# Attention kernel: key tiles in six sets of 2, 3, 3, 2, 3 and 3 in place of eight pairs, stack loads issued behind a set's last tile

## The chip, the core and the metric

One core of a Trainium2 chip runs the program. The metric is the device time of one execution in microseconds. TensorE (PE in the rows; its weight loads PEld) multiplies, VectorE (DVE) and ScalarE (ACT) read its results from the eight PSUM banks, GpSimd (POOL) adds tiles, SyncE (SP), ACT and POOL issue DMAs.

## What is computed

```python
xn = layernorm(x)                      # x: 4 x 2048 x 512
q, k, v = heads(xn @ Wq.T + bq)/sqrt(32), heads(xn @ Wk.T + bk), heads(xn @ Wv.T + bv)   # 16 heads of 32
attn = softmax(q @ k.T)                # 2048 x 2048 for each of 4 * 16 = 64 heads
att = (attn @ v) @ Wo.T + bo
ffn = tanh(xn @ W @ A1 @ A2 + b)
out = x + att + ffn
```

## The kernel before

Three stages follow each other: the weights, the projections (queries and keys split in two parts of reduced precision and stacked on 96 rows, written to DRAM), and attention, `build_attend`, which the change is in. The attention of 64 heads takes most of the time. PE runs them in a loop of four heads per turn (15 turns) and the last four written out.

**The work of a head.** The 2048 keys are 16 key tiles of 128 (`kt`, 0 to 15), the 2048 queries four blocks of 512 (`q`). `scores` (L1122) computes a tile's scores for one block into one of three banks (`st_bank`); ACT takes their exponential into a tile `probs` (`exps`, L901). `use` (L1128) multiplies a whole exponential tile by the values into `pv_bank`, with weights of 32 columns, four blocks spread over the array's four column strips; the scores use 128 columns. So PE alternates between a stretch of 128-column score matmuls and a stretch of 32-column ones.

**The row maximum.** The exponential needs each query's maximum beforehand. `max_scores` (L1095) computes the scores a second time, queries on the rows, for a head that comes later, into one of four banks (`sm_bank`); DVE reduces each bank to a column (`maxima`, L999: a *read* below). A head has 64 such units, numbered `k`. The two kinds stand in turn: for each tile and block `both_scores` issues one maximum matmul, then one score matmul. The maxima run four tiles ahead: at tiles 0 to 11 stand units 16 to 63 of the next head, at tiles 12 to 15 units 0 to 15 of the head after. After unit 63 DVE reduces the columns to `row_max` (L1016), PE turns it (`turn_max`, L1104), DVE negates it (`negate`, L970) and SP loads it as row 97 of the query stack.

**The banks.** The table `SM_TURN` deals the units, the turned maximum (`"max"`) and the bank of the row sums (`"sum"`) to the four banks in turn; a maximum matmul waits until DVE has read what its bank held before, four places earlier (`sm_before`). A score matmul waits for the exponential three units earlier (`st_units_before`), one place being left free (`ST_SKIP`) and one for DVE's scaling (`SPARE_AFTER`: unit 2 of each head waits for `context_ready`).

**The order on PE.** Tiles go in pairs: the scores (with maxima) of two tiles, 8 maxima and 8 scores in turn, then `use` of the two tiles before:

```python
for p in range(CUT // 2, (KT if more >= 2 else END_TILE) // 2):
    both_scores(h, r, 2 * p, to_turn, more)
    both_scores(h, r, 2 * p + 1, to_turn, more)
    use(h, r, 2 * p - 2)
    use(h, r, 2 * p - 1)
```

After tiles 8 and 9 of the next head, `add_up` sums a head's exponentials over the keys. They have been added before: some tiles by POOL (L827), some by DMAs that POOL issues and that add to `dma_sum` (`join`, L838; `merge`, L846). ACT copies the sums and the product (`copy_sums`, `copy_pv`, L908); DVE inverts the sums after a head's 64 maxima (`invert`, L975 and L978) and scales after unit 15 (`scale`, L982 and L987). ACT also issues the loads of stacks three heads ahead (`load`, L299 and L305), one each after tiles 6, 7, 9, 10, 12, 13 and 15 (`LOAD_AT`).

Of the kernel before, what the change touches and what calls it, by code (L numbers as in the profile page):

```python
# [26 lines left out]
KT = SEQ // P  # L27
# [3 lines left out]
GROUP = 4  # L31
ROWS = 3 * DH
MROW = ROWS
SM_BANKS, ST_BANKS = 4, 3
UNITS = KT * QB
PER_TILE = UNITS // KT
AHEAD = 4
TURN_UNIT = 8
BEGIN = 16
SUM_UNIT = 56  # L40
SCALED = 15
ST_SKIP, ST_SLOTS = 24, 66
CUT = 10
LOAD_AT = [6, 7, 9, 10, 12, 13, 15]


CHAINS = [[0, 2, 5, 8, 10, 13]]
# [9 lines left out]
END_TILE = 12  # L57
# [5 lines left out]
LAST_CONTEXT = (BATCH - 1) * TB  # L63


SM_TURN = [*range(TURN_UNIT), "max", *range(TURN_UNIT, SUM_UNIT), "sum", *range(SUM_UNIT, UNITS), None, None]


MAX_FROM = 10
# [24 lines left out]
def sm_place(what):  # L94
    return SM_TURN.index(what) % SM_BANKS

# [29 lines left out]
SPARE_BEFORE = max(u for u in range(UNITS) if st_place(u) == spare_place())  # L126
SPARE_AFTER = min(u for u in range(UNITS) if st_place(u) == spare_place())

assert ST_SKIP % (2 * PER_TILE) == 0 and ST_SLOTS % ST_BANKS == 0 and SCALED + 1 == AHEAD * PER_TILE
assert UNITS == 64 and len(SM_TURN) % SM_BANKS == 0 and st_slot(UNITS - 1) == ST_SLOTS - 2  # L130


# [502 lines left out]
def build_attend(nc, dram, out, first):  # L635
# [3 lines left out]
    with ExitStack() as own:  # L639
# [241 lines left out]
        @block.scalar  # L881
        def _(act):
            for s in (probs_ready, pv_copied, sums_copied):
                act.sem_inc(s, PRIME)

            def exps(h, r, kt):

                for q in range(QB):
                    if q == 0 and kt in SLOT:
                        old, back = tile_before(kt)  # L890
                        act.wait_ge(tile_used, PRIME + h * KT - back * KT + old + 1)
                        if not back and isinstance(h, int) and h == LAST:
                            if old in LAST_POOL:
                                act.wait_ge(pool_added, PRIME + h * POOL_ADDS + max(1, LAST_POOL.index(old)))
                        elif old in POOL_TILES:
                            act.wait_ge(pool_added, PRIME + h * POOL_ADDS - back * POOL_ADDS + adds_after(old))
                        elif old != kt and not (back and isinstance(h, int) and h == 0):
                            before, place = (h - 1, (r + 1) % 2) if back else (h, r % 2)
                            act.wait_ge(joined[place], landed(before, CHAINS[0].index(old)))
                    act.wait_ge(scores_ready, h * UNITS + kt * QB + q + 1)  # L900
                    nc.scalar.activation(tile_at(r, kt)[:, q * BLK:(q + 1) * BLK],  # L901
                                         score_bank(h, kt * QB + q), ACT.Exp,
                                         scale=SCALE).then_inc(probs_ready, 1)

            def copy_bank(h, r, bank, copies, ready, value, copied):
                act.wait_ge(ready, value)
                act.wait_ge(context_ready, PRIME + h - 1)
                nc.scalar.activation(copies[r % 2][:], bank[:], ACT.Copy).then_inc(copied, 1)  # L908

            def copy_pv(h, r):  # L910
                copy_bank(h, r, pv_bank, pv_copy, tile_used, PRIME + h * KT + KT, pv_copied)

            def copy_sums(h, r):
                bank = last_sum if isinstance(h, int) and h == LAST else sum_bank
                copy_bank(h, r, bank, sum_copy, sums_ready, PRIME + h + 1, sums_copied)

            def high(n, par):
                act.wait_ge(ctx_loaded[par], (n // 2) * DMA + DMA)
                act.wait_ge(res_ready, PRIME + n * JT - JT)
                nc.scalar.activation(ctx_hi[par], ctx_in[par], ACT.Copy).then_inc(hi_ready, 1)  # L920

            def load(h, r, i):

                if i < len(PARTS):
                    load_part(act, dram, h, i, q_st[r], k_st[r], head_loaded[r])
                elif r % 2:
                    load_v(act, dram, h - 1, v_sb[r // 2], v_loaded[r // 2])

            for kt in range(CUT):
                exps(0, 0, kt)  # L930
                if kt == LOAD_AT[0]:
                    act.wait_ge(first["v_stored"], V_STORED)
                if kt in LOAD_AT:
                    load(GROUP - 1, GROUP - 1, LOAD_AT.index(kt))

            def body(h, r, more, following):
                for kt in range(CUT, KT):
                    exps(h, r, kt)
                    if kt in LOAD_AT and more >= GROUP - 1:
                        load(h + GROUP - 1, (r + GROUP - 1) % GROUP, LOAD_AT.index(kt))  # L940
                if more:
                    for kt in range(CUT):
                        exps(following, (r + 1) % GROUP, kt)
                        if kt == 1:
                            copy_pv(h, r)
                        if kt in LOAD_AT and more >= GROUP:
                            load(h + GROUP, r, LOAD_AT.index(kt))
                        if kt == CUT - 1:
                            copy_sums(h, r)
                else:  # L950
                    copy_pv(h, r)
                    high(2, 0)
                    high(3, 1)
                    copy_sums(h, r)

            heads(act, body)
            for n in range(4, EARLY_BLOCKS + 2):
                high(n, n % 2)
            block_pairs(act, lambda n, par, ahead: high(n + 2, par), EARLY_BLOCKS, BLOCKS - 2)

        @block.vector
        def _(dve):
# [30 lines left out]
            def maxima(s, k, units, sums_of):  # L993

                if units:
                    if k == 0:
                        dve.wait_ge(row_max_ready, PRIME + s)
                    dve.wait_ge(max_scores_ready, s * UNITS + k + 1)
                    nc.vector.tensor_reduce(part_max[:, k:k + 1], sm_bank[:, sm_place(k)], AX.X,  # L999
                                            ALU.max).then_inc(max_scores_read, 1)  # L1000
                if k == SCALED and sums_of is not None:
                    scale_in_spare(*sums_of)

# [4 lines left out]
                        negate(s - 1)  # L1008
                    maxima(s, k, units, sums_of)

            def rest(s, units=True, sums_of=None):
                for k in range(BEGIN, UNITS):
                    maxima(s, k, units, sums_of)
                if units:
                    dve.wait_ge(max_scores_read, PRIME + s * UNITS + UNITS)
                    nc.vector.tensor_reduce(row_max[:], part_max[:].rearrange("p (q b) -> p q b", b=QB), AX.X,  # L1016
                                            ALU.max).then_inc(row_max_ready, 1)
                if sums_of is not None:
                    invert(*sums_of)

            dve.sem_inc(max_row_ready, 1)
            rest(1)
# [20 lines left out]

            def body(h, r, more, following):
                if more >= 3:
                    rest(following + 1, sums_of=(h, r))
                    begin(following + 2, sums_of=(h, r))
                elif more == 2:
                    rest(following + 1)
# [28 lines left out]
        def _(pe):  # L1078
# [100 lines left out]
                    scores(h, r, kt, q)  # L1179

            pe.sem_inc(turned_ready, 1)
            for p in range(CUT // 2):
                both_scores(0, 0, 2 * p, 1, 2)
                both_scores(0, 0, 2 * p + 1, 1, 2)
                if p:
                    use(0, 0, 2 * p - 2)
                    use(0, 0, 2 * p - 1)

            def end_of_heads():

# [12 lines left out]
            def body(h, r, more, following, to_turn):  # L1203
                if more == 0:
                    return
                r1 = (r + 1) % GROUP
                for p in range(CUT // 2, (KT if more >= 2 else END_TILE) // 2):
                    both_scores(h, r, 2 * p, to_turn, more)
                    both_scores(h, r, 2 * p + 1, to_turn, more)
                    use(h, r, 2 * p - 2)  # L1210
                    use(h, r, 2 * p - 1)
                if more == 1:
                    end_of_heads()
                if more >= 2:
                    for p in range(CUT // 2):
                        both_scores(following, r1, 2 * p, to_turn + 1, more - 1)
                        both_scores(following, r1, 2 * p + 1, to_turn + 1, more - 1)
                        if p == 0:
                            use(h, r, KT - 2)
                            use(h, r, KT - 1)  # L1220
                        else:
                            use(following, r1, 2 * p - 2)
                            use(following, r1, 2 * p - 1)
                        if p == CUT // 2 - 1:
                            add_up(h, r, more)

            def output_part(n, par, j):
                pe.wait_ge(res_ready, PRIME + n * JT + j - JT + 1)
# [92 lines left out]
```

## Time and profile before

| | us |
|---|---|
| median of 3 executions | 4086.81 |
| lowest and highest | 4084.3, 4092.52 |
| the profiled execution | 4089.26 |
| its span in the trace | 4087.4 |

TensorE's granted clock is 0.998 of full over the span. The span's last instruction ends 1.9 us short of the profiled execution's time. In the trace a timeline row gives start, duration, engine, line, operation, tile written and read, and a count where like instructions were merged; in brackets stands the idle time before and what ended it. PE's matmuls are pipelined, so the distance between two starts is their cost, not the duration shown.

### The profile page before, as it was taken

To read this page: it belongs to the slowest core of one execution; us is meant where nothing else is said; L and a number is where in the kernel's file an instruction comes from. 1 tells how busy PE (TensorE), PEld (TensorE's weight loads), DVE (VectorE), ACT (ScalarE), POOL (GpSimd) and SP (SyncE) were. 2 spreads that over 40 slices of the span, in tenths; PEclk is the share of its full clock that TensorE was granted. 3 is DMA by queue.
4 is the path that set the end of the run, shared out by engine and by line. 5 is a ranking of instruction groups with operands and counts; after the bars stand their busy time and mean duration, and the time that the engine had idled before them with its cause. 6 is when DMAs were issued, how large, how long until landed. Compare 5 with 4: busy or idle time off the path is not lost.

```text
span 4087.4 us, 77851 instructions
## 1 busy us (share of the span) xinstructions
PE 4044.5 (99%) x21280; PEld 2493.3 (61%) x21280; DVE 3075.7 (75%) x5122; ACT 2367.1 (58%) x4515; POOL 3164.7 (77%) x1108
## 2 busy tenths in 40 slices
PE   8999999999999999999999999999999999999999
PEld 6888888755555555555555555555555555555477
DVE  4344333788888888888888888888888888888734
ACT  2222122167677677777676777776776767676621
POOL 1222222289999999999999999999999999999920
PEclk9999999999999999999999999999999999999999
DMA  4444444568888888888888888888888888888767
GB/s 173 157 170 159 153 151 159 174 148 168 176 180 176 179 170 179 173 177 174 175 178 178 176 175 175 174 171 174 178 179 178 171 176 175 177 175 177 171 211 257
DMA packets 245348, 714.80 MB, mean 175 GB/s; under 512 B 87281, under 2 KB 88305, under 8 KB 184433
## 3 DMA queue, kind: packets, MB, share of 16 engines
q0 software_dynamic: 54288, 395.34, 49.9%
q1 hardware_dynamic: 107648, 201.88, 14.5%
q10 hardware_dynamic: 83040, 113.01, 10.2%
q8 instruction: 186, 3.05, 0.3%
q14 instruction: 186, 1.52, 0.1%
HBM read 178.00 MB, written 136.31 MB: 77 GB/s over the span
## 4 chain that ended last, share of the span: by engine, by line
PE 63%; DMA 11%; issue 4%; POOL 2%; ACT 1%; POOLq 0%; ACTq 0%; DVE 0%; DVEq 0%
PE sm_bank L1095 20%; PE st_bank L1122 18%; PE pv_bank L1128 18%; DMA dma_sum<-pool_sum 6%; DMA dma_sum<-probs 5%; PE sm_bank L289 3%; POOL pool_sum L827 2%; PE sm_bank L1128 2%; PE st_bank L289 1%; ACT probs L901 1%; PE sm_bank L1104 0%; PE sm_bank L1122 0%; DMA q_stack<-max_row 0%; POOL dma_sum L838 0%; ACTq L900 0%
## 5 line engine op out<-in xcount | busy, mean ns | idle before, releaser
L999 DVE TENSOR_REDUCE part_max<-sm_bank 128x1 f32<-128x512 f32 x4016 | 2448.3, 682 | 368.1 <-PE sm_bank L1095 365.9
L827 POOL TENSOR_TENSOR pool_sum<-pool_sum,probs 128x2048 f32<-128x2048 f32 x504 | 2467.6, 4896 | 20.2 <-DMA dma_sum<-probs 3.7
L901 ACT ACTIVATE probs<-st_bank 128x512 f32<-128x512 f32 x3810 | 1947.9, 616 | 575.6 <-PE st_bank L1122 557.5
L1095 PE MATMUL sm_bank<-k_stack,q_stack 96*128 96x512 f32 x4016 | 1662.0, 414 | 15.4 <-issue 13.0
L1122 PE MATMUL st_bank<-q_stack,k_stack 97*128 97x512 f32 x4064 | 1619.7, 400 | 1.5 <-DMA q_stack<-max_row 1.5
L1095 PEld LDWEIGHTS sm_bank<-k_stack,q_stack 96*128 96x128 f32 x4016 | 761.7, 190 | 589.4 <-DVE part_max L999 371.5
L1128 PE MATMUL pv_bank<-probs,v_pairs 128*32 128x512 f32 x7680 | 931.2, 598 | 0.0
L1122 PEld LDWEIGHTS st_bank<-q_stack,k_stack 97*128 97x128 f32 x4064 | 772.4, 190 | 195.8 <-ACT probs L901 25.9
L1128 PEld LDWEIGHTS pv_bank<-probs,v_pairs 128*32 128x32 f32 x7680 | 202.6, 109 | 452.2 <-ACT probs L901 255.8
L838 POOL DMA_DIRECT2D dma_sum<-probs x315 | 345.8, 1098 | 99.8 <-DMA dma_sum<-probs 46.0
L433 POOL TENSOR_TENSOR y_out<-y_out,x_in 128x512 f32<-128x512 f32 x64 | 82.8, 1293 | 370.2 <-ACT y_out L465 365.7
L827 POOL TENSOR_TENSOR pool_sum<-probs 128x2048 f32<-128x2048 f32 x63 | 326.4, 5181 | 0.1
L459 ACT ACTIVATE qk_hi<-proj,qk_bias 128x512 fp32r<-128x512 f32 x128 | 88.1, 688 | 272.3 <-PE proj L289 272.3
L552 DVE SCALAR_TENSOR_TENSOR qk_lo<-proj,qk_bias,qk_hi 128x512 fp32r<-128x512 f32 x128 | 96.1, 751 | 195.6 <-ACT qk_hi L459 193.8
L465 ACT ACTIVATE y_out<-y_out 128x512 f32<-128x512 f32 x64 | 40.5, 633 | 319.6 <-DVE y_out L541 319.6
L901 ACT ACTIVATE dma_sum<-st_bank 128x512 f32<-128x512 f32 x254 | 137.3, 595 | 128.3 <-PE st_bank L1122 127.8
L422 POOL TENSOR_TENSOR rstd<-rstd,power 128x4 f32<-128x4 f32 x15 | 15.3, 1017 | 189.9 <-DVE rstd L487 189.9
L541 DVE TENSOR_TENSOR y_out<-proj,row_bias 128x512 f32<-128x512 f32 x64 | 44.3, 692 | 121.8 <-PE proj L289 121.8
L908 ACT ACTIVATE sum_copy<-sm_bank 128x512 f32<-128x512 f32 x64 | 38.2, 597 | 146.9 <-PE sm_bank L1128 146.9
L530 DVE TENSOR_TENSOR v_out<-proj,row_bias 128x512 f32<-128x512 f32 x64 | 44.2, 691 | 104.7 <-PE proj L289 104.7
L289 PE MATMUL proj<-q_stack,w_hi 128*128 128x512 f32 x256 | 101.6, 397 | 2.2 <-DVEq L566 2.2
L289 PE MATMUL proj<-w_hi,xt_hi 128*128 128x512 f32 x256 | 102.5, 401 | 0.0
(130 smaller groups left out, 3231.2 us busy)
## 6 DMA issues: line engine op xcount, KB each, us to landing
dma_sum<-probs POOLq DMA_DIRECT2D x315, 1024.0 KB, 8.3
dma_sum<-pool_sum POOLq DMA_DIRECT2D x62, 1024.0 KB, 10.2
q_stack<-s_q_hi ACTq DMA_DIRECT2D x122, 256.0 KB, 7.5
k_stack<-s_k_hi ACTq DMA_DIRECT2D x122, 256.0 KB, 4.5
x_in<-in_x SPq DMA_DIRECT2D x16, 1024.0 KB, 7.7
s_q_hi<-qk_hi SPq DMA_DIRECT2D x16, 1024.0 KB, 4.3
s_q_lo<-qk_lo SPq DMA_DIRECT2D x16, 1024.0 KB, 6.4
s_k_hi<-qk_hi SPq DMA_DIRECT2D x16, 1024.0 KB, 4.3
```

The lines of the kernel that those rows point to most:

```text
L289: last = nc.tensor.matmul(out, a(c), b(c), start=(c == 0 and n == 0), stop=(c == CT - 1 and n == 2))
L433: nc.gpsimd.tensor_tensor(y_out[:, j], y_out[:, j], x_in[par][:, j], ALU.add).then_inc(half_y, 1)
L459: nc.scalar.activation(qk_hi[:, t, g], proj[:, u % RING], ACT.Identity, bias=keep["qk_bias"][:, t, g:g + 1]).then_inc(hi_ready, 1)
L541: nc.vector.tensor_tensor(y_out[:, j], proj[:, u % RING], keep["row_bias"][:, 1], ALU.add).then_inc(proj_free, 1)
L552: nc.vector.scalar_tensor_tensor(qk_lo[:, t, g], proj[:, u % RING], keep["qk_bias"][:, t, g:g + 1], qk_hi[:, t, g].bitcast(F32), ALU.add, ...
L827: nc.gpsimd.tensor_tensor(total[:], one[:], tile_at(r, kt)[:], ALU.add).then_inc(pool_added, 1)
L838: nc.gpsimd.dma_start(dma_sum[r % 2][:], tile_at(r, CHAINS[0][j])[:], accum_op=ALU.add).then_inc(joined[r % 2], DMA)
L901: nc.scalar.activation(tile_at(r, kt)[:, q * BLK:(q + 1) * BLK], score_bank(h, kt * QB + q), ACT.Exp, scale=SCALE).then_inc(probs_ready, 1)
L999: nc.vector.tensor_reduce(part_max[:, k:k + 1], sm_bank[:, sm_place(k)], AX.X, ALU.max).then_inc(max_scores_read, 1)
L1095: nc.tensor.matmul(sm_bank[:, sm_place(k)], q_st[r][0:ROWS, q * P:(q + 1) * P], k_st[r][0:ROWS, b * BLK:(b + 1) * BLK], start=True, stop=T ...
L1122: nc.tensor.matmul(score_bank(h, u), k_st[r][0:ROWS + 1, kt * P:(kt + 1) * P], q_st[r][0:ROWS + 1, q * BLK:(q + 1) * BLK], start=True, sto ...
L1128: last = nc.tensor.matmul(bank[q * DH:(q + 1) * DH, :], left, right[:, q * BLK:(q + 1) * BLK], start=start, stop=stop)
```

## The change

The pairs become `TILE_SETS`. A set's scores are issued for all its tiles in a row, then the `use` of the set before. The table of banks has its free places elsewhere, the turned maximum stands ahead of unit 4 (tile 13) where it stood ahead of unit 8 (tile 14), `invert` runs after unit 3 where it ran after `row_max`, and the seven loads are issued in four places. `add_up` keeps its place behind tile 9.

```diff
-TURN_UNIT = 8
+TURN_UNIT = 4
-SCALED = 15
-ST_SKIP, ST_SLOTS = 24, 66
+INVERTED, SCALED = 3, 15
+ST_SKIP, ST_SLOTS = 32, 66
 CUT = 10
-LOAD_AT = [6, 7, 9, 10, 12, 13, 15]
+TILE_SETS = [[0, 1], [2, 3, 4], [5, 6, 7], [8, 9], [10, 11, 12], [13, 14, 15]]
+SET_ENDS = [tiles[-1] + 1 for tiles in TILE_SETS]
+CUT_SET = SET_ENDS.index(CUT) + 1
+LOAD_AT = {1: [0], 4: [1, 2], 12: [3, 4], 15: [5, 6]}
...
-SM_TURN = [*range(TURN_UNIT), "max", *range(TURN_UNIT, SUM_UNIT), "sum", *range(SUM_UNIT, UNITS), None, None]
+SM_TURN = [*range(TURN_UNIT), "max", *range(TURN_UNIT, 24), None, *range(24, 36), None, *range(36, SUM_UNIT), "sum",
+           *range(SUM_UNIT, UNITS)]
...
             def body(h, r, more, following):
                 for kt in range(CUT, KT):
                     exps(h, r, kt)
-                    if kt in LOAD_AT and more >= GROUP - 1:
-                        load(h + GROUP - 1, (r + GROUP - 1) % GROUP, LOAD_AT.index(kt))
+                    for i in LOAD_AT.get(kt, []) if more >= GROUP - 1 else []:
+                        load(h + GROUP - 1, (r + GROUP - 1) % GROUP, i)
...
+                if k == INVERTED and sums_of is not None:
+                    invert(*sums_of)
                 if k == SCALED and sums_of is not None:
                     scale_in_spare(*sums_of)
...
-            def rest(s, units=True, sums_of=None):
+            def rest(s, units=True):
...
-                if sums_of is not None:
-                    invert(*sums_of)
...
-                for p in range(CUT // 2, (KT if more >= 2 else END_TILE) // 2):
-                    both_scores(h, r, 2 * p, to_turn, more)
-                    both_scores(h, r, 2 * p + 1, to_turn, more)
-                    use(h, r, 2 * p - 2)
-                    use(h, r, 2 * p - 1)
+                if more >= 2:
+                    for i in range(CUT_SET, len(TILE_SETS)):
+                        for kt in TILE_SETS[i]:
+                            both_scores(h, r, kt, to_turn, more)
+                        for kt in TILE_SETS[i - 1]:
+                            use(h, r, kt)
...
                 if more >= 2:
-                    for p in range(CUT // 2):
-                        both_scores(following, r1, 2 * p, to_turn + 1, more - 1)
-                        both_scores(following, r1, 2 * p + 1, to_turn + 1, more - 1)
...
+                    for i, tiles in enumerate(TILE_SETS[:CUT_SET]):
+                        for kt in tiles:
+                            both_scores(following, r1, kt, to_turn + 1, more - 1)
+                        for kt in TILE_SETS[i - 1]:
+                            if i == 0:
+                                use(h, r, kt)
+                            else:
+                                use(following, r1, kt)
+                    add_up(h, r, more)
```

DVE, around the end of a head's maxima, in the part of the program behind the loop; the rows begin with the 48 reads of units 16 to 63. Before:

```order
L999 TENSOR_REDUCE part_max<-sm_bank 128x1 x48
L1016 TENSOR_REDUCE row_max<-part_max 128x16
L975 TENSOR_REDUCE totals<-sum_copy 128x16
L978 RECIPROCAL inverse<-totals 128x16
L999 TENSOR_REDUCE part_max<-sm_bank 128x1 x8
L970 TENSOR_SCALAR max_row<-sm_bank 16x128
L999 TENSOR_REDUCE part_max<-sm_bank 128x1 x8
L982 STREAM_TRANSPOSE st_bank<-inverse 128x512
```

The same place of the changed kernel:

```order
L1003 TENSOR_REDUCE part_max<-sm_bank 128x1 x48
L1022 TENSOR_REDUCE row_max<-part_max 128x16
L1003 TENSOR_REDUCE part_max<-sm_bank 128x1 x4
L979 TENSOR_REDUCE totals<-sum_copy 128x16
L982 RECIPROCAL inverse<-totals 128x16
L974 TENSOR_SCALAR max_row<-sm_bank 16x128
L1003 TENSOR_REDUCE part_max<-sm_bank 128x1 x12
L986 STREAM_TRANSPOSE st_bank<-inverse 128x512
```

The two steps of `invert` have moved behind four reads and stand directly ahead of the negation, and twelve reads follow the negation where eight did.

ACT, from tile 10 on, at the same place of the program; a tile is four exponentials. Before:

```order
L901 ACTIVATE probs<-st_bank 128x512 x4
L299 DMA k_stack<-s_k_hi 32x2048
L901 ACTIVATE probs<-st_bank 128x512 x8
L299 DMA k_stack<-s_k_hi 32x2048
L901 ACTIVATE probs<-st_bank 128x512 x4
L299 DMA k_stack<-s_k_lo 32x2048
L901 ACTIVATE probs<-st_bank 128x512 x8
L305 DMA v_pairs<-s_v 128x16x64
```

And of the changed kernel:

```order
L905 ACTIVATE probs<-st_bank 128x512 x12
L303 DMA k_stack<-s_k_hi 32x2048 x2
L905 ACTIVATE probs<-st_bank 128x512 x12
L303 DMA k_stack<-s_k_lo 32x2048
L309 DMA v_pairs<-s_v 128x16x64
```

No load stands between two tiles of a set any more; they stand behind tiles 12 and 15, two at a time.

## Rows read from the trace of the kernel before

**Rows 1.** Windows: each engine's busy us and instructions, PEclk, DMA share, GB/s.

```profile
1000.00:2000.00 1000.00, 994.46 (x5498) 556.31 (x5495) 863.01 (x1453) 703.26 (x1369) 967.73 (x313) 1.00 0.84 175
```

**Rows 2.** Timeline of PE: `use` of tiles 0 and 1, then tiles 4 and 5.

```profile
2083.15 1.07 PE L1128 MATMUL pv_bank<-dma_sum,v_pairs 128*32 128x512 f32 x8
2084.03 1.04 PE L1128 MATMUL pv_bank<-probs,v_pairs 128*32 128x512 f32 x8
2085.00 0.50 PE L1095 MATMUL sm_bank<-k_stack,q_stack 96*128 96x512 f32 x1
2085.34 0.40 PE L1122 MATMUL st_bank<-q_stack,k_stack 97*128 97x512 f32 x1
...
2088.62 0.39 PE L1122 MATMUL st_bank<-q_stack,k_stack 97*128 97x512 f32 x1
2088.94 1.92 PE L1128 MATMUL pv_bank<-probs,v_pairs 128*32 128x512 f32 x16
2090.79 0.50 PE L1095 MATMUL sm_bank<-k_stack,q_stack 96*128 96x512 f32 x1
```

**Rows 3.** Timeline of PE: the pair of tiles 0 and 1 of the same head.

```profile
2073.03 0.50 PE L1095 MATMUL sm_bank<-k_stack,q_stack 96*128 96x512 f32 x1
...
2076.42 0.39 PE L1122 MATMUL st_bank<-q_stack,k_stack 97*128 97x512 f32 x1
2076.68 0.50 PE L1095 MATMUL sm_bank<-k_stack,q_stack 96*128 96x512 f32 x1
2077.02 0.40 PE L1122 MATMUL st_bank<-q_stack,k_stack 97*128 97x512 f32 x1
...
2079.20 0.50 PE L1095 MATMUL sm_bank<-k_stack,q_stack 96*128 96x512 f32 x1
```

**Rows 4.** Timeline of DVE from tile 10 of that head on.

```profile
2056.16 4.88 DVE L999 TENSOR_REDUCE part_max<-sm_bank 128x1 f32<-128x512 f32 x8 [2.35 <-PE sm_bank L1095]
2061.08 0.22 DVE L1016 TENSOR_REDUCE row_max<-part_max 128x16 f32<-128x64 f32 x1
2061.21 0.70 DVE L975 TRANSPOSE_TENSOR_REDUCE totals<-sum_copy 128x16 f32<-128x512 f32 x1
2061.95 0.25 DVE L978 RECIPROCAL inverse<-totals 128x16 f32<-128x16 f32 x1
2062.15 4.88 DVE L999 TENSOR_REDUCE part_max<-sm_bank 128x1 f32<-128x512 f32 x8
2067.54 0.28 DVE L970 TENSOR_SCALAR max_row<-sm_bank 16x128 fp32r<-16x128 f32 x1 [0.51 <-PE sm_bank L1104]
2067.78 4.88 DVE L999 TENSOR_REDUCE part_max<-sm_bank 128x1 f32<-128x512 f32 x8
2072.57 0.72 DVE L982 STREAM_TRANSPOSE st_bank<-inverse 128x512 f32<-128x512 f32 x1
2073.54 0.69 DVE L987 TENSOR_TENSOR ctx_out<-pv_copy,st_bank 128x512 f32<-128x512 f32 x1 [0.25 <-DVE st_bank L982]
2074.15 4.87 DVE L999 TENSOR_REDUCE part_max<-sm_bank 128x1 f32<-128x512 f32 x8
...
2085.54 4.88 DVE L999 TENSOR_REDUCE part_max<-sm_bank 128x1 f32<-128x512 f32 x8 [0.92 <-PE sm_bank L1095]
```

**Rows 5.** Timeline of ACT: the exponentials of tiles 4 and 5.

```profile
2085.78 4.03 ACT L901 ACTIVATE probs<-st_bank 128x512 f32<-128x512 f32 x8 [1.77 <-PE st_bank L1122]
```

**Rows 6.** Timeline of PE: add_up of two heads that follow each other.

```profile
2054.63 1.06 PE L1128 MATMUL sm_bank<-dma_sum,ones 128*32 128x512 f32 x8 [0.38 <-DMA dma_sum<-pool_sum]
...
2102.46 1.06 PE L1128 MATMUL sm_bank<-dma_sum,ones 128*32 128x512 f32 x8
```

**Rows 7.** Waits from 1000 to 3800 us: waiter, releaser, us, times, longest.

```profile
PE sm_bank L1095 <- issue: 9.7, 12, 1.1
PE sm_bank L1128 <- DMA dma_sum<-pool_sum: 6.5, 18, 0.8
```

**Rows 8.** DMA issues of the page: count, KB each, us to landing.

```profile
dma_sum<-pool_sum POOLq DMA_DIRECT2D x62, 1024.0 KB, 10.2
```

More of the change, by code:

```diff
@@ L127 @@
 SPARE_AFTER = min(u for u in range(UNITS) if st_place(u) == spare_place())
-assert ST_SKIP % (2 * PER_TILE) == 0 and ST_SLOTS % ST_BANKS == 0 and SCALED + 1 == AHEAD * PER_TILE
+assert ST_SKIP // PER_TILE in SET_ENDS and CUT in SET_ENDS and SUM_UNIT == (CUT + AHEAD) * PER_TILE and ST_SLOTS % ST_BANKS == 0 and SCALED + 1 == AHEAD * PER_TILE
 assert UNITS == 64 and len(SM_TURN) % SM_BANKS == 0 and st_slot(UNITS - 1) == ST_SLOTS - 2
@@ L930, in _ @@
                 exps(0, 0, kt)
-                if kt == LOAD_AT[0]:
+                if kt == min(LOAD_AT):
                     act.wait_ge(first["v_stored"], V_STORED)
-                if kt in LOAD_AT:
-                    load(GROUP - 1, GROUP - 1, LOAD_AT.index(kt))
+                for i in LOAD_AT.get(kt, []):
+                    load(GROUP - 1, GROUP - 1, i)
             def body(h, r, more, following):
@@ L943, in body @@
                         exps(following, (r + 1) % GROUP, kt)
-                        if kt == 1:
+                        if kt == TILE_SETS[0][-1]:
                             copy_pv(h, r)
-                        if kt in LOAD_AT and more >= GROUP:
-                            load(h + GROUP, r, LOAD_AT.index(kt))
+                        for i in LOAD_AT.get(kt, []) if more >= GROUP else []:
+                            load(h + GROUP, r, i)
                         if kt == CUT - 1:
@@ L1009, in begin @@
                     maxima(s, k, units, sums_of)
[L1011 removed]
+            def rest(s, units=True):
                 for k in range(BEGIN, UNITS):
[L1013 removed]
+                    maxima(s, k, units, None)
                 if units:
@@ L1045, in body @@
                 if more >= 3:
-                    rest(following + 1, sums_of=(h, r))
+                    rest(following + 1)
                     begin(following + 2, sums_of=(h, r))
@@ L1181, in _ @@
             pe.sem_inc(turned_ready, 1)
-            for p in range(CUT // 2):
[L1183 to L1187, printed above, removed]
+            for i, tiles in enumerate(TILE_SETS[:CUT_SET]):
+                for kt in tiles:
+                    both_scores(0, 0, kt, 1, 2)
+                for kt in TILE_SETS[i - 1] if i else []:
+                    use(0, 0, kt)
             def end_of_heads():
@@ L1206, in body @@
                 r1 = (r + 1) % GROUP
-                for p in range(CUT // 2, (KT if more >= 2 else END_TILE) // 2):
-                    both_scores(h, r, 2 * p, to_turn, more)
-                    both_scores(h, r, 2 * p + 1, to_turn, more)
-                    use(h, r, 2 * p - 2)
-                    use(h, r, 2 * p - 1)
+                if more >= 2:
[4 more added lines that the diff above has]
+                            use(h, r, kt)
                 if more == 1:
+                    for kt in range(CUT, END_TILE):
+                        both_scores(h, r, kt, to_turn, more)
+                    for kt in TILE_SETS[CUT_SET - 1]:
+                        use(h, r, kt)
                     end_of_heads()
                 if more >= 2:
-                    for p in range(CUT // 2):
-                        both_scores(following, r1, 2 * p, to_turn + 1, more - 1)
-                        both_scores(following, r1, 2 * p + 1, to_turn + 1, more - 1)
[L1218 to L1225, printed above, removed]
+                    for i, tiles in enumerate(TILE_SETS[:CUT_SET]):
+                        for kt in tiles:
+                            both_scores(following, r1, kt, to_turn + 1, more - 1)
+                        for kt in TILE_SETS[i - 1]:
+                            if i == 0:
+                                use(h, r, kt)
+                            else:
+                                use(following, r1, kt)
+                    add_up(h, r, more)
             def output_part(n, par, j):
```

## Prediction

> **What bounds the kernel now.** I read first the busy times of 1000 us in the middle of the attention [rows 1]: PE has work for 994 of them at full clock (1.00, the 2.4 GHz level), POOL for 968, DVE for 863, ACT for 703. PE is the bound, and its busy time hides what a matmul costs, so next comes its timeline, start to start. In a plain pair the scores follow each other at 3.28/14 = 0.234 us (from 2085.34 to 2088.62, 14 steps), and the tile of `use` costs 0.88 (2083.15 to 2084.03). The pair takes 2090.79 - 2085.00 = 5.79 us [rows 2]. Sixteen scores at 0.234 are 3.74, two tiles at 0.88 are 1.76; what is left, **0.29 us, is the change of kind**, there and back. A head takes 2102.46 - 2054.63 = 47.83 us from one `add_up` to the next [rows 6]; some 62 heads go that way, since there are 62 merges [rows 8]. The rest is no concern of the change.
>
> **The second thing to see is how close DVE is.** Its eight reads last 4.88 us, so they start every (4.88 - 0.68)/7 = 0.60 us if the last lasts 0.68, and in a row of runs without a pause the next instruction starts 4.79 us later, or 8 times 0.60 (2067.78 to 2072.57) [rows 4]. PE makes a bank for it every 2 x 0.234 = 0.467 us. Within a set PE is thus the faster one, and DVE catches up only while PE does `use`: it idles 0.92 us before a plain pair. Its first read starts 0.54 us after the set's first matmul (2085.54 against 2085.00) [rows 2, 4]. There are four banks, so maximum matmul number m of a set (from 0) waits for read m - 4.
>
> What such a wait costs on PE is shown by the pair of tiles 0 and 1, where DVE is late by its scaling: reads from 2074.15, the third ends at 2074.15 + 1.20 + 0.68 = 2076.03, the fourth at 2076.63. The last two scores start at 2076.42 and 2077.02, **0.39 behind those ends**, and the pair takes 6.17 in place of 5.79, that is 0.38 more [rows 3, 4].
>
> **The change, part by part.**
>
> (a) *Six sets for eight.* Two changes of kind fewer in a head: 2 x 0.29 = -0.58 us. A rule of the Trainium skill speaks for this part: TensorEngine Tiling (Array Packing), section Key Properties, says that changing the tiling mode, not just the tile, drains TensorE. The trace agrees that the alternation has a price, the 0.29 us above.
>
> (b) *Twelve reads in a row.* In a set of three tiles PE would start score number 11 at 0.34 + 11 x 0.467 = 5.48 after the set's start. Maximum matmul 11 waits for read 7, which ends at 0.54 + 7 x 0.60 + 0.68 = 5.42; the score behind it starts 0.39 later, at 5.81. So the set is 0.33 us longer than its matmuls. The same sum for m = 8 gives 3.62 + 0.39 = 4.01 against an unhindered 4.08, so it begins at m = 9 only; a pair ends at m = 7 and never sees it. The trace of before has no row of twelve reads; the nearest row is [rows 3]. Bounds: nothing, if PE's loads of weights hid it all, and 0.6, one read, if each wait cost a whole one; I take 0.33, by the rule that rows 3 follow to 0.01. For the sets [2,3,4], [5,6,7] and [10,11,12]: 3 x 0.33 = +0.99. The Trainium skill warns of this kind of thing: its page Trainium Kernel Development and Optimization, Best Practices, says "Mind PSUM pressure: TensorE tiling speeds up compute but not PSUM evacuation". The trace agrees: 0.467 us a bank on PE, 0.60 on DVE.
>
> (c) *The set [13,14,15].* Here DVE comes late too, and nothing has made up for it. In the set before, tiles 10 to 12, it does eight reads (0.54 to 5.46), then `row_max`, 0.22, then it must wait for that before unit 0 (0.04 us where DVE waits on its own small results, as between 2061.91 and 2061.95; 0.25 behind the write to PSUM [rows 4]; I take 0.04), so four reads from 5.72, and at 8.12 `invert`: 2062.15 - 2061.21 = 0.94. Negation starts at 9.06 and the first read 0.24 later at 9.30 [rows 4]. PE has by then started the set: 0.34 + 11 x 0.467 + 0.33 (late) and from the last score on 2090.79 - 2088.62 = 2.17 for two tiles of `use`, 7.98, and 0.03 for the turn, 8.01. First read 1.29 behind the start, in place of 0.54: read 7 ends at 1.29 + 4.2 + 0.68 = 6.17, the last score starts at 6.56, against 5.48: **+1.08**. If `invert` hid nothing of itself but came ahead of other work, as before, this would be +0.33, and if the wait on `row_max` costs 0.25, +1.29.
>
> (d) *Tiles 0 and 1.* The scaling comes behind the twelfth read, at 1.29 + 7.2 = 8.49 after the start of [13,14,15]; it and its gap take 2074.15 - 2072.57 = 1.58, and reads go on from 10.07. PE starts tile 0 at 6.56 + 2.17 + 0.88 = 9.61, the third tile of `use` in it, so the first read comes 0.46 after the set's start: no delay, and the 0.38 of now are gone. Unit 2's score finds `context_ready` in time as well. **-0.38**. The twelfth read's lateness is thus paid in one set and not in two.
>
> (e) *The loads.* ACT has 1.77 us idle before a plain pair and its exponentials follow at (4.03 - 0.60)/7 = 0.49 [rows 5]. From 0.78 after the set's start, exponential 8 ends at some 5.3 and the last score waits for it until 5.4 at most: not the one that binds, since (b) holds it until 5.81. Loads behind a set's last tile fall in that idle time and cost PE nothing; kept clear of tiles 5 to 11 they leave the merge alone, which lands 10.2 us after its issue [rows 8] and for which `add_up` waited 0.38 us in one head of the two shown and 6.5 us in all over 2800 us [rows 6, 7]. With every head longer, POOL (968 of 1000 us) comes earlier as well. I count -0.1 a head, half of it for waits that sit in weight loads and don't show as PE's idle; between 0 and -0.2. The loop's own gap, 9.7 us in 12 turns [rows 7], stays.
>
> **Sum.** -0.58 + 0.99 + 1.08 - 0.38 - 0.1 = +1.01 us a head. Some waits that PE has now (one head in four comes 0.6 to 1 us behind the others by the loop's gap) will overlap with those of (c), for which I take off 0.15: **+0.86 x 62 = +53 us**. The profiled execution took 4089.26, the median is 4086.81, 2.4 less: 4087 + 53 = 4140.
>
> **Rivals.**
>
> 1. *The stalls stay hidden and the sets pay.* (b) and (c) cost nothing: PE has 64 banks' work per head and DVE 0.60 x 64 = 38.4 us of reads and some 2.9 of other work (0.14 + 0.94 + 0.24 + 1.58) in 47.8, so there is room on average. Then -0.58 - 0.38 - 0.1 = -1.06 a head, but POOL needs 0.968 x 48 = 46.5 and becomes a second bound just under that, so perhaps -0.9: -56 us, 4031; with the switches alone, 4087 - 36 = 4051. Against it: four banks are 4 x 0.467 = 1.9 us of lead, and the lag grows by 0.133 a read from a margin of 0.6 at m = 4; rows 3 show PE held already in a pair when DVE starts 0.6 late. Chance 0.12.
>
> 2. *Half of it.* The stall of (b) comes in all four sets, but `invert` runs while DVE would have idled in `use`, so that (c) is 0.33: -0.58 + 1.32 - 0.38 - 0.1 = +0.26, +16 us, 4103. For it: PE's `use` behind tile 12 gives DVE 1.8 us. Against: by the count above DVE has read its twelfth bank just when PE is done. Chance 0.14.
>
> 3. *ACT is late as well.* Its three banks are as narrow, and it is held in a set of three by the exponentials' wait for their tile buffer, which POOL and the chain of adding DMAs free. Each set of three then loses another 0.3 or so: +1.2 a head, +75 us, 4215. It decides where exponential 8 ends later than 5.4 us into a set; by rows 5 it has 0.1 before that and 0.5 with DVE's delay. Chance 0.06, with a half-way case (4170 to 4190) of 0.05.
>
> 4. *The change doesn't do what it says*, the sets being broken up by some other wait of the program: nothing in the order of DVE or ACT speaks for it; within the others.
>
> **How the numbers follow.** The forecast case, 4140, has 0.63 and by the bounds of (b), (c) and (e) reaches from 4112 to 4166: 0.1 us on each of four sets moves it by 25 us. To hold 8 in 10 the range takes in the half case from 4098 on, and up to 4172. What a measurement of this kernel can tell from no change is some 0.2%, 8 us. Faster by more than that: rival 1, 0.12. Within it: 0.04, the edge between rivals 1 and 2. Slower: 0.84.
>
> **What would show it.** In the changed profile: PE's last score of a plain set of three some 5.8 us after its first matmul, with starts 0.60 apart at the end and DVE without a pause through its twelve reads; at tiles 13 to 15 the last score at 6.5; the pair of tiles 0 and 1 without a wait; a head of about 48.7 to 49.0 us; more waits of PE's weight loads on `part_max`; the wait on `dma_sum<-pool_sum` gone. Wrong would be the forecast if scores stayed 0.234 apart through a set of three (rival 1), if the first read of tile 13 came less than 0.7 after the set's start (rival 2), or if score matmuls waited on ACT in sets of three (rival 3).

## The result, and the profile after

The changed kernel takes 4123.19 us (median of 4, 4121.89 to 4124.72), the kernel before 4086.51 beside it: a ratio of 1.0088, 95% interval 1.0070 to 1.0105, **slower by 0.9%, some 37 us**. Forecast was 4140 in a range from 4098 to 4172. The span of the profiled execution went from 4087.4 to 4120.1 us.

Windows, 1000 us of the attention, changed kernel, columns as in [rows 1]:

```profile
1000.00:2000.00 1000.00, 999.82 (x5440) 534.21 (x5438) 852.31 (x1444) 703.15 (x1359) 958.90 (x309) 1.00 0.83 174
```

PE counts as busy for 999.8 us of 1000, against 994.5 in [rows 1], and yet it issued 58 matmuls fewer (5440 against 5498). Hardly any idle time stands between its matmuls, but they start further apart. Where, its timeline shows. A set of three tiles (5, 6 and 7) and the three tiles of `use` behind it:

```profile
2001.92 0.50 PE L1099 MATMUL sm_bank<-k_stack,q_stack 96*128 96x512 f32 x1
2002.26 0.39 PE L1126 MATMUL st_bank<-q_stack,k_stack 97*128 97x512 f32 x1
...
2006.01 0.39 PE L1126 MATMUL st_bank<-q_stack,k_stack 97*128 97x512 f32 x1
2006.23 0.46 PE L1099 MATMUL sm_bank<-k_stack,q_stack 96*128 96x512 f32 x1
2006.53 0.40 PE L1126 MATMUL st_bank<-q_stack,k_stack 97*128 97x512 f32 x1
2006.79 0.50 PE L1099 MATMUL sm_bank<-k_stack,q_stack 96*128 96x512 f32 x1
2007.13 0.39 PE L1126 MATMUL st_bank<-q_stack,k_stack 97*128 97x512 f32 x1
2007.39 0.50 PE L1099 MATMUL sm_bank<-k_stack,q_stack 96*128 96x512 f32 x1
2007.73 0.39 PE L1126 MATMUL st_bank<-q_stack,k_stack 97*128 97x512 f32 x1
2008.05 2.78 PE L1132 MATMUL pv_bank<-probs,v_pairs 128*32 128x512 f32 x24
2010.76 0.50 PE L1099 MATMUL sm_bank<-k_stack,q_stack 96*128 96x512 f32 x1
```

Up to the ninth score (L1126, 2006.01) the matmuls of both kinds follow each other at 0.234 us as in [rows 2], so the scores at 0.467; the last three scores start at 2006.53, 2007.13 and 2007.73, 0.60 apart, which is DVE's pace. The last one starts 5.81 us after the set's first matmul.

DVE over the same stretch and the set of tiles 13 to 15 behind it, to compare with [rows 4]:

```profile
2002.46 7.27 DVE L1003 TENSOR_REDUCE part_max<-sm_bank 128x1 f32<-128x512 f32 x12 [0.71 <-PE sm_bank L1099]
...
2024.09 2.48 DVE L1003 TENSOR_REDUCE part_max<-sm_bank 128x1 f32<-128x512 f32 x4
2026.49 0.70 DVE L979 TRANSPOSE_TENSOR_REDUCE totals<-sum_copy 128x16 f32<-128x512 f32 x1
2027.23 0.25 DVE L982 RECIPROCAL inverse<-totals 128x16 f32<-128x16 f32 x1
2027.40 0.21 DVE L974 TENSOR_SCALAR max_row<-sm_bank 16x128 fp32r<-16x128 f32 x1
2027.54 7.24 DVE L1003 TENSOR_REDUCE part_max<-sm_bank 128x1 f32<-128x512 f32 x12
2034.71 0.70 DVE L986 STREAM_TRANSPOSE st_bank<-inverse 128x512 f32<-128x512 f32 x1
```

From 2024.09 to the scaling at 2034.71 DVE doesn't pause. PE meanwhile, in the set of tiles 13 to 15 (its scores counted from 0):

```profile
2026.26 0.28 PE L1108 MATMUL sm_bank<-ident,row_max 128*16 128x128 f32 x1
2026.30 0.48 PE L1099 MATMUL sm_bank<-k_stack,q_stack 96*128 96x512 f32 x1
...
2028.60 0.39 PE L1126 MATMUL st_bank<-q_stack,k_stack 97*128 97x512 f32 x1
...
2032.78 0.39 PE L1126 MATMUL st_bank<-q_stack,k_stack 97*128 97x512 f32 x1
2033.10 2.78 PE L1132 MATMUL pv_bank<-probs,v_pairs 128*32 128x512 f32 x24
2035.82 0.50 PE L1099 MATMUL sm_bank<-k_stack,q_stack 96*128 96x512 f32 x1
```

DVE's first read starts 1.24 after the set's first matmul (2027.54 against 2026.30); from score 4 at 2028.60 on PE's scores come every 4.18/7 = 0.60 us, and the last score starts 6.48 after the first matmul. Between 1000 and 3800 us, waits of PE's weight loads for a read are more and shorter (924 in place of 565), and the waits for the merge are as good as gone (6.5 us of PE before, [rows 7]). The first row is of the kernel before, the other two of the changed one:

```profile
PEld sm_bank L1095 <- DVE part_max L999: 348.5, 565, 0.8
PEld sm_bank L1099 <- DVE part_max L1003: 294.7, 924, 0.8
...
PE sm_bank L1132 <- DMA dma_sum<-pool_sum: 0.2, 1, 0.2
```

The total of this wait fell although PE lost time, so it doesn't measure the loss; the starts do. From the starts of matmuls between 1000 and 3700 us I took, for some 55 heads of each kernel, the median distance from one set's first matmul to the next (us, in the order of the program; the kernel before has 16 tiles in eight pairs), and the mean head:

| | add_up | 10.. | 12.. or 13.. | 14.. | 0.. | 2.. | 4.. or 5.. | 6.. | 8.. | mean head |
|---|---|---|---|---|---|---|---|---|---|---|
| before | 1.00 | 5.80 | 5.83 | 5.77 | 6.17 | 5.79 | 5.79 | 5.87 | 5.70 | 48.22 |
| changed | 0.97 | 8.02 | 9.53 | | 6.65 | 7.99 | 8.84 | | 6.54 | 48.64 |

All tables below are made in this way.

### The profile page after: what moved, and what is told of

Its sections match the earlier page's. It is cut to its first block, busy times and chain, and to the rows that moved or that the text cites. A ratio compares the mean times of both kernels' runs of the same rounds, so it can differ in the third digit from the quotient of the medians.

```text
span 4120.1 us, 77851 instructions
## 1 busy us (share of the span) xinstructions
PE 4088.8 (99%) x21280; PEld 2445.1 (59%) x21280; DVE 3064.2 (74%) x5122; ACT 2383.0 (58%) x4515; POOL 3166.3 (77%) x1108
## 4 chain that ended last, share of the span: by engine, by line
PE 78%; DMA 1%; issue 0%; POOL 0%; DVE 0%; ACT 0%; ACTq 0%; POOLq 0%; DVEq 0%
PE sm_bank L1099 27%; PE st_bank L1126 23%; PE pv_bank L1132 22%; PE sm_bank L293 3%; PE sm_bank L1132 1%; PE st_bank L293 1%; DMA dma_sum<-probs 1%; POOL pool_sum L831 0%; PE sm_bank L1108 0%; DMA dma_sum<-pool_sum 0%; PE sm_bank L1126 0%; ACT probs L905 0%; DVE part_max L1003 0%; DVE probs L1039 0%; ACTq L904 0%
## 5 line engine op out<-in xcount | busy, mean ns | idle before, releaser
L905 ACT ACTIVATE probs<-st_bank 128x512 f32<-128x512 f32 x3810 | 1970.7, 628 | 447.7 <-PE st_bank L1126 431.7
L1099 PE MATMUL sm_bank<-k_stack,q_stack 96*128 96x512 f32 x4016 | 1729.1, 431 | 7.5 <-issue 4.8
L1126 PE MATMUL st_bank<-q_stack,k_stack 97*128 97x512 f32 x4064 | 1612.9, 398 | 5.9 <-ACT probs L905 5.4
L1132 PE MATMUL pv_bank<-probs,v_pairs 128*32 128x512 f32 x7680 | 905.3, 597 | 0.0
L1126 PEld LDWEIGHTS st_bank<-q_stack,k_stack 97*128 97x128 f32 x4064 | 770.6, 190 | 177.7 <-ACT probs L905 54.2
L1132 PEld LDWEIGHTS pv_bank<-probs,v_pairs 128*32 128x32 f32 x7680 | 215.4, 109 | 496.7 <-issue 291.9
L842 POOL DMA_DIRECT2D dma_sum<-probs x315 | 318.1, 1010 | 133.8 <-PE pv_bank L1132 113.5
L831 POOL TENSOR_TENSOR pool_sum<-probs 128x2048 f32<-128x2048 f32 x63 | 309.7, 4916 | 0.1
L912 ACT ACTIVATE pv_copy<-pv_bank 128x512 f32<-128x512 f32 x64 | 38.3, 598 | 131.3 <-PE pv_bank L1132 131.3
```

The source lines that it names most:

```text
L831: nc.gpsimd.tensor_tensor(total[:], one[:], tile_at(r, kt)[:], ALU.add).then_inc(pool_added, 1)
L842: nc.gpsimd.dma_start(dma_sum[r % 2][:], tile_at(r, CHAINS[0][j])[:], accum_op=ALU.add).then_inc(joined[r % 2], DMA)
L1099: nc.tensor.matmul(sm_bank[:, sm_place(k)], q_st[r][0:ROWS, q * P:(q + 1) * P], k_st[r][0:ROWS, b * BLK:(b + 1) * BLK], start=True, stop=T ...
L1126: nc.tensor.matmul(score_bank(h, u), k_st[r][0:ROWS + 1, kt * P:(kt + 1) * P], q_st[r][0:ROWS + 1, q * BLK:(q + 1) * BLK], start=True, sto ...
L1132: last = nc.tensor.matmul(bank[q * DH:(q + 1) * DH, :], left, right[:, q * BLK:(q + 1) * BLK], start=start, stop=stop)
```

## The experiments

**What each part does by itself.** The first four ran on one chip with the kernel before (4085.34 us). *Loads alone:*

```diff
-LOAD_AT = [6, 7, 9, 10, 12, 13, 15]
+LOAD_AT = {1: [0], 4: [1, 2], 12: [3, 4], 15: [5, 6]}
...
```

> The kernel before with one part of the change alone: the loads in their new places (behind tiles 1, 4, 12 and 15), pairs and bank table as before. Theory L, the old places of the loads cost PE something: the merge lands late for add_up (it landed 10.2 us after its issue, 8.3 in the changed kernel) and the loop's gap of 0.8 us in one head of four comes from a load just ahead of it. Then the mean head goes from 48.22 to about 47.8 us, the gap in front of the first matmul of a loop turn is gone, and the time is 4060 (4055 to 4070). Theory S, those waits went only because the heads of the changed kernel are longer and POOL has more time: 4087 within 8, with the gap kept.

Measured: **4233.79**, a ratio of 1.0369 (1.0351 to 1.0386). Neither theory's time came. ACT's timeline, tiles 4 and 5, with the two loads behind tile 4:

```profile
2045.30 2.07 ACT L901 ACTIVATE probs<-st_bank 128x512 f32<-128x512 f32 x4 [1.63 <-PE st_bank L1122]
2046.77 0.32 ACTq L299 DMA_DIRECT2D q_stack<-s_q_lo  x1
2047.19 1.17 ACTq L299 DMA_DIRECT2D q_stack<-s_q_hi  x1
2048.62 2.06 ACT L901 ACTIVATE probs<-st_bank 128x512 f32<-128x512 f32 x4 [1.25 <-PE st_bank L1122]
```

and PE, at the last score of that pair:

```profile
2047.91 0.39 PE L1095 MATMUL sm_bank<-k_stack,q_stack 96*128 96x512 f32 x1
2049.27 0.50 PE L1122 MATMUL st_bank<-q_stack,k_stack 97*128 97x512 f32 x1 [0.97 <-ACT probs L901]
```

The first issue takes 0.32 us and the second, right behind it, 1.17; ACT's next exponential stands behind it in the queue, and the score that needs the bank waits. That pair takes 7.02 us in place of 5.79, and tiles 12 and 13, with the other double issue in their middle, 6.28 in place of 5.83. Besides, the small load of the maximum's row is late for tile 0: it is issued 5.2 us before that tile, as in the kernel before, but takes 6.5 us to land in place of 4.1 (medians), and PE waits for it, 52.6 us over 2800:

```profile
PE st_bank L1122 <- DMA q_stack<-max_row: 52.6, 38, 2.2
```

so tiles 0 and 1 take 7.03. The changed kernel has both covers: its double issues fall behind a set's end, and its maximum is turned a tile earlier, so that the row's load, with 6.1 us to landing, is issued 8.2 us ahead of tile 0. *Sets with the old loads:*

```diff
-LOAD_AT = {1: [0], 4: [1, 2], 12: [3, 4], 15: [5, 6]}
+LOAD_AT = {6: [0], 7: [1], 9: [2], 10: [3], 12: [4], 13: [5], 15: [6]}
```

> The changed kernel with the loads back in their old places (one each behind tiles 6, 7, 9, 10, 12, 13 and 15). Theory L: the mean head goes from 48.64 to about 49.0, the loop's gap of 0.8 us is back, the time is 4145 (4135 to 4152). Theory S: 4123 within 8.

Measured: 4131.15 (4125.78 to 4131.49), ratio 1.0113, mean head 48.75 against the changed kernel's 48.64. By the mean heads the loads' place is worth 0.1 us a head in the sets, so neither 4145 nor quite nothing (4131 is at the edge of theory S, and its ratio's interval, 1.0097 to 1.0130, overlaps that of the changed kernel); and the loop's gap of L's account is not back. *The sets undone, all else as changed:*

```diff
-TILE_SETS = [[0, 1], [2, 3, 4], [5, 6, 7], [8, 9], [10, 11, 12], [13, 14, 15]]
+TILE_SETS = [[kt, kt + 1] for kt in range(0, KT, 2)]
```

> The changed kernel with the sets undone: eight pairs, all else as changed (bank table, turned maximum ahead of unit 4, invert after unit 3, loads). By the count from starts of reads and matmuls: no set with twelve reads, pairs of 5.79 us, but invert now stands in the middle of the pair of tiles 12 and 13 and holds unit 7's matmul until the negation: that pair 0.94 longer, tiles 0 and 1 again 6.17. A head 47.7 + 0.94 = 48.6, the time about 4115 (4105 to 4125), near the changed kernel's by another road. Rival, the sets' long rows of reads are not what costs: then it is slower than the changed kernel by two changes of kind, 0.58 us a head, 4159.

Measured: 4182.61, ratio 1.0237, outside both expectations. The pair of tiles 12 and 13 takes 6.63 (I had 6.73 for it), tiles 0 and 1 6.18 as expected; what I had left out is the pair of tiles 4 and 5 at 7.02, the double issue again. With it, 1.2 us a head, the count comes to 4115 + 75 = 4190. Tiles 0 and 1 are not held here by the maximum's row, which is turned a tile earlier. *Loads at the ends of pairs,* all else as before:

```diff
-LOAD_AT = [6, 7, 9, 10, 12, 13, 15]
+LOAD_AT = {1: [0], 3: [1, 2], 13: [3, 4], 15: [5, 6]}
...
```

> The kernel before with the loads behind a pair's last tile: 0 behind tile 1, 1 and 2 behind tile 3, 3 and 4 behind 13, 5 and 6 behind 15. Theory L: as with the new places, 4060 (4053 to 4068), all loads out of a pair's middle and away from the merge. Theory S: 4087 within 8.

Measured: **4067.52**, ratio 0.9953 (0.9937 to 0.9970), mean head 47.79. Kept clear of the merge and of a pair's middle, the loads' new times are worth 0.43 us a head in pairs. The merge takes hardly less time to land (9.6 us after its issue, 10.2 before), but it is issued earlier: 17.15 us after the start of tile 0 in place of 19.0, by the median over the heads. With it went POOL's waits for the landing of the DMAs that add (`join`): 46.0 us over 2800 in the kernel before, 8.9 now. In the kernel before the merge landed, by the median, 0.05 us ahead of `add_up`, with nothing to spare; now it is 2.5 us, and PE's wait for it no longer stands among the waits.

**Is it the second issue, or any load in a pair's middle?**

```diff
-LOAD_AT = [6, 7, 9, 10, 12, 13, 15]
+LOAD_AT = {1: [0], 3: [1], 4: [2], 12: [3], 13: [4], 14: [5], 15: [6]}
...
```

> The kernel before with one load each behind tiles 1, 3, 4, 12, 13, 14 and 15: no two in a row, three of them in a pair's middle, none near the merge. Theory Q: what made the pairs with the new places slow (4234) is the second of two load issues in a row, which holds ACT for 0.5 to 1.5 us and in a pair's middle holds the exponentials of the second tile. Then this is as fast as the loads at pair ends, 4067 (4060 to 4078), a mean head of 47.8 to 47.9. Rival, it is any load in a pair's middle at tiles 4 and 12: above 4150.

Measured: 4072.16 (ratio 0.9963), mean head 47.87. Three loads in a pair's middle cost next to nothing when each stands alone. So it is the second in a row that holds tiles 4 and 5. And 0.35 of the 0.43 us are kept, so they come mainly of loads clear of the merge and not of loads clear of a pair's middle.

**Is it DVE that holds the sets of three?** Half reads in both kernels, so that the maxima leave out half of the keys:

```diff
-                    nc.vector.tensor_reduce(part_max[:, k:k + 1], sm_bank[:, sm_place(k)], AX.X,
+                    nc.vector.tensor_reduce(part_max[:, k:k + 1], sm_bank[:, sm_place(k), 0:BLK // 2], AX.X,
```

> The changed kernel with DVE reading half of each bank (256 of 512 columns), so the maxima are over half of the keys only. It takes DVE away as a cause. Theory D, the sets of three are held by DVE's pace: scores stay 0.234 apart to the end, a set of three with two tiles of use takes 7.65 us and not 7.99, tiles 13 to 15 take 8.5 and not 9.53, a head is 46.7 to 47.3 by what POOL allows, the time 4020 to 4045. If the stalls are of another making: unchanged, 4123.

> The kernel before with DVE reading half of each bank, likewise. Theory D: only tiles 0 and 1 gain, 0.38 us a head, so a head of 47.8 and 4063 (4055 to 4080), slower than the sets with half reads by up to two changes of kind, 0.58 us a head or 36 us, unless POOL holds both.

Measured: 4039.5 with sets (ratio 0.9897 to the kernel before) and 4063.07 with pairs (0.9948). The order turns round: **with DVE out of the way the six sets are the faster ones, by 24 us** (three times each: 4036.84, 4039.50 and 4051.51 against 4061.12 to 4063.29).

| | 10.. | 12.. or 13.. | 0.. | 2.. | 4.. or 5.. | 8.. | mean head |
|---|---|---|---|---|---|---|---|
| sets, half reads | 7.71 | 8.50 | 6.65 | 7.78 | 8.53 | 7.17 | 47.37 |
| pairs, half reads | 5.79 | 5.83 | 5.79 | 5.79 | 5.79 | 6.04 | 47.76 |

A set of three with three tiles of `use` falls from 8.84 to 8.53, tiles 13 to 15 from 9.53 to 8.50, tiles 0 and 1 in pairs from 6.17 to 5.79. Not all of it arrives. Tiles 2 to 4 take 7.78 where 7.65 was expected: there the scores start 0.49 us apart, the pace of ACT's exponentials (eleven in 5.50 us), and the last one starts 5.58 after the first matmul. Tiles 8 and 9 now take 7.17, since the merge comes late. Waits of PE itself, 1000 to 3800 us, sets with half reads:

```profile
PE sm_bank L1132 <- DMA dma_sum<-pool_sum: 24.0, 37, 1.0
```

POOL, which must add a head's tiles before the merge, is busy for 983 us of 1000 here and so probably the next bound; no run lightened it.

**Is the set of tiles 13 to 15 late by `invert`?**

```diff
-INVERTED, SCALED = 3, 15
+INVERTED, SCALED = 15, 15
```

> The changed kernel with invert behind unit 15, just ahead of the scaling. Theory D by the starts of reads and matmuls: tiles 13 to 15 take 8.84 and not 9.53 us, for the first read is at 0.54 again; tiles 0 and 1 take 7.3 and not 6.65, for the scaling ends 0.94 later. Net nothing: 4121 (4113 to 4129). If the lateness of tiles 13 to 15 is not the work of invert, that set keeps 9.53 and the time rises to 4160.

Measured: 4128.72 (4127.74 to 4129.69), at the upper edge. Tiles 13 to 15 take 8.83, and tiles 0 and 1 7.47 in place of 6.65. DVE:

```profile
2028.11 7.26 DVE L1003 TENSOR_REDUCE part_max<-sm_bank 128x1 f32<-128x512 f32 x12
2035.30 0.70 DVE L979 TRANSPOSE_TENSOR_REDUCE totals<-sum_copy 128x16 f32<-128x512 f32 x1
2036.03 0.25 DVE L982 RECIPROCAL inverse<-totals 128x16 f32<-128x16 f32 x1
2036.39 0.73 DVE L986 STREAM_TRANSPOSE st_bank<-inverse 128x512 f32<-128x512 f32 x1
2037.37 0.69 DVE L991 TENSOR_TENSOR ctx_out<-pv_copy,st_bank 128x512 f32<-128x512 f32 x1 [0.26 <-DVE st_bank L986]
```

PE began tile 0 at 2036.41, in the middle of this. The 0.94 us of `invert` cost about the same in either place (16.30 us for the two sets, 16.18 in the changed kernel); DVE has no spare time in either.

**One pair of sets of three by itself.** Loads at the ends (the second and third now behind tile 4), the maxima's bank table and `invert` as before; the free place of the score banks is the changed kernel's (`ST_SKIP` 32). Against its partner with pairs the change is this:

```diff
-ST_SKIP, ST_SLOTS = 24, 66
+ST_SKIP, ST_SLOTS = 32, 66
...
+TILE_SETS = [[0, 1], [2, 3, 4], [5, 6, 7], [8, 9], [10, 11], [12, 13], [14, 15]]
...
-LOAD_AT = {1: [0], 3: [1, 2], 13: [3, 4], 15: [5, 6]}
+LOAD_AT = {1: [0], 4: [1, 2], 13: [3, 4], 15: [5, 6]}
...
```

> Loads at pair ends, bank table and invert as before, and only tiles 2 to 7 in two sets of three in place of three pairs. By the count: one change of kind fewer, -0.29 us a head, two sets whose last matmuls wait for reads, 2 x 0.33. A mean head of 47.79 + 0.3 = 48.1, the time 4067 + 20 = 4087 (4080 to 4092). Rival, sets of three pay where DVE comes to them on time: 47.5 and 4049.

Measured: 4105.01 with a wide spread (4094.67 to 4110.09), so it ran again, beside its partner with pairs:

> The same kernel as one_pair_of_threes, whose times spread from 4094.7 to 4110.1 while its profiled execution was near 4094 to 4095. If its trace is the rule (a mean head of 48.10 us), the median here is 4092 to 4098, and against the pairs with loads at pair ends of the same call +0.3 us a head, 19 us, and a few more at the ends of the program.

> The partner, the same kernel as pairs_loads_at_pair_ends: 4063 to 4071, a ratio of 0.995 to the kernel before.

Measured: 4096.18 and 4064.02 (ratios 1.0025, 1.0015 to 1.0035, and 0.9947, 0.9933 to 0.9960): two sets of three in place of three pairs, with what goes with them, cost 32 us. The two sets take 7.98 and 8.85 us, tiles 8 and 9 6.54 for the third tile of `use`, together 23.37; the four pairs of the partner 5.86 + 5.79 + 5.79 + 5.68 = 23.12. The mean head is 48.10 in the first trace and 48.20 in the second against 47.79, so 19 to 26 us lie in the heads; of the rest 3 us are a longer stop where the loop ends (below), and the remaining few are not accounted for.

**A faster version.** Two costs of the kernel before stand apart from the sets: the loads' places, and the 0.38 us at tiles 0 and 1. On top of the loads at pair ends, DVE's scaling is split, the transposition ahead of the read of unit 15 and the product behind it:

```diff
+                if k == SCALED and sums_of is not None:
+                    h, r = sums_of
+                    dve.wait_ge(probs_ready, PRIME + h * UNITS + UNITS + SPARE_BEFORE + 1)
+                    spread_ratio(h, r, st_bank[:, spare_place()])
                 if units:
...
```

> The kernel with loads at pair ends, with DVE's scaling split: the transposition (L982) ahead of the read of unit 15, the product behind it. The 0.25 us that the product waits for the transposition is then filled by the read, and DVE reaches tiles 0 and 1 some 0.3 us earlier: that pair 5.85 to 5.95 us in place of 6.17, a head 47.5, the time 4050 (4045 to 4060). If POOL (47.5 us of a head between its first adds in the kernel before) is by now the bound, the gain is not seen in the time but stands as a wait of PE on the merge or of ACT on pool_sum: 4067.

Measured: **4047.65** (4042.77 to 4050.12), ratio 0.9898 (0.9880 to 0.9916): 1% faster than the kernel before. Tiles 0 and 1 take 5.80 us, the mean head 47.40. DVE fills the gap with the read and starts tile 0 on time:

```profile
2006.42 0.72 DVE L982 STREAM_TRANSPOSE st_bank<-inverse 128x512 f32<-128x512 f32 x1
2007.05 0.65 DVE L1006 TENSOR_REDUCE part_max<-sm_bank 128x1 f32<-128x512 f32 x1
2007.62 0.67 DVE L991 TENSOR_TENSOR ctx_out<-pv_copy,st_bank 128x512 f32<-128x512 f32 x1
2008.23 4.88 DVE L1006 TENSOR_REDUCE part_max<-sm_bank 128x1 f32<-128x512 f32 x8
```

POOL is busy there for 983 us of 1000, against 968 in [rows 1], so little is probably left to gain on PE alone; no run tested that.

## Why the prediction was right, and where it was off

**(a) The change of kind, -0.58 us a head: borne out.** With half reads a set of three with three tiles of `use` takes 8.53 us; 24 matmuls of scores and maxima at 0.234, three tiles at 0.88 and one change of kind at 0.29 make 8.55. Over the head the sets gain 0.39 us (47.37 against 47.76), since ACT's pace and the merge take part of it back. The gain is there; with whole reads it is overrun.

**(b) The twelfth read, +0.33 a set: right to 0.02.** Sets of 8.02 (with the turn) and 7.99 us were forecast as 8.01 and 7.98; the one with three tiles of `use`, 8.84, is 7.98 + 0.88 = 8.86 by the same count. The half reads show that it is DVE and not the length of the set. Rival 1 was right that the average leaves DVE room (it is busy for 852 us of 1000) and wrong that this is enough: DVE holds PE in every set of three, because four banks don't carry the lag. Rival 3, ACT late as well, didn't come either: the last scores of a set start 0.60 apart and not 0.49. With half reads ACT's pace does show, in tiles 2 to 4, so it comes next there.

**(c) Tiles 13 to 15, +1.08: 1.01 measured** (last score at 6.49 by the median against 5.48). The count had DVE's first read at 1.29 and it was at 1.25. Rival 2, with 0.33 for this set, is refuted, and moving `invert` showed that it is its 0.94 us which come too late.

**(d) Tiles 0 and 1 without a wait: right.** A plain pair with a third tile of `use` is 5.79 + 0.88 = 6.67; measured 6.65.

**(e) The sum: the step that was mis-sized is what it was set against.** The forecast for a head of the changed kernel, 47.83 + 0.86 = 48.69 us, is right to 0.05: the mean is 48.64. But 47.83 is one clean head of the kernel before, whose mean is 48.22: waits for the merge, a longer `add_up` at the loop's turn (1.18 us by the mean, 1.00 by the median) and slower pairs in some heads lie between the two, and the changed kernel has hardly any of them. I took 0.25 us off for such waits, though the head that I had read held only some 0.1 of them (47.83 against 47.72, the sum of the medians above), and then multiplied by 62 as if the others had none more. From the mean the same count gives +0.47; measured is **+0.42 us a head**. Of the 33 us that the span grew, 62 heads at 0.42 are 26. Another 7 come from one place that I hadn't seen: behind the loop's end ACT stops once for 5.58 us in the changed kernel (2.08 in the kernel before), and PE with it:

```profile
3802.16 2.16 ACT L905 ACTIVATE probs<-st_bank 128x512 f32<-128x512 f32 x4 [5.58 <-issue]
```

A head there takes 55.5 us, against 47.9 in the kernel before. Sets with the old loads (52.4), pairs with single loads (51.5) and with loads at pair ends (53.3) lose time there as well; pairs with half reads and the old loads (47.4, with a stop of 1.98) and pairs with the changed loads (48.8, with none) don't. So neither the sets nor the loads' places explain it. What ACT waits for there no view says, and no run was made for it.

That 4123 fell so near 4140 is thus in part luck: without this stop, which the prediction doesn't have, the kernel would be some 30 us slower (an estimate: 37 less 7) against a forecast of 53.

**The loads, read as harmless: right for this kernel, for a reason that I had only half.** I had them fall into ACT's idle time behind a set's last tile. They do, and must: the second of two issues in a row can hold ACT for a time that the kernel before, with single loads, never showed. Why the waits for the merge went in the changed kernel has two answers that both count. In pairs the loads' places did it (0.43 us a head). In sets with the old loads, PE itself waits 3.2 us for the merge over 2800 and its weight loads 25.9 (42.0 in the kernel before), so there the longer heads do most of it and the loads' places are worth 0.1.

What stays open: the gap of 0.8 us at the loop's turn ([rows 7], 12 times). Each of three edits by itself takes it out of the waits or nearly so: the loads elsewhere in pairs (at pair ends, singly, or doubled), half reads in pairs, and the sets with the old loads (0.6 us left). Part of what the loads' places gain in pairs is this gap: the mean `add_up` went from 1.18 to 0.97 us. Why three such different edits remove it is not known.

## What to carry to other kernels

A producer that is the bound in total can still be held, stretch by stretch, by a consumer with time to spare: count its lead in banks against the difference of the two paces over the longest uninterrupted row (here 0.60 against 0.467 us a bank, four banks, good for eight reads and not for twelve). Make the sum from the mean of the repeated stretch and not from the clean one, since the clean one lacks the very waits that a slower version will swallow. And where two DMA issues stand in a row on an engine that also computes, look at what stands behind the second.

## What the runs showed of the hardware

- A load issue on ACT takes 0.32 us alone. The second of two that follow at once took longer, but not always: between 1000 and 3700 us of the run with the loads alone it took 1.16 us by the median behind tile 4 (`q_stack`, 52 of 53 over 0.6 us) and 0.38 behind tile 12 (`k_stack`, 12 of 54 over 0.6, the longest 1.48). Everything behind it in ACT's queue waits, which goes with the 1.2 us of tiles 4 and 5 and the 0.45 of tiles 12 and 13. What makes it long no run shows. In the kernel before, with single issues, the longest of this load was 0.35 us.
- DVE's reads of a bank start 0.60 us apart, in rows of eight and of twelve, and a dependent DVE instruction behind a transposition into PSUM starts 0.25 us after its end; another DVE instruction in between fills that gap for nothing (2006.42 to 2008.23, 1.81 us with a read of 0.60 in it, where 1.58 and 0.60 stood one behind the other).
- Reads of 256 columns keep PE's pace, eight in 3.70 us or one every 0.467, where reads of 512 start every 0.60.
